# Keys and values stored to DRAM as whole fp32, split in two on GpSimd after they are read back

## The reference

```python
for n in (1, 2):
    h = layer_norm(x)
    q = h @ wq + bq;  k = ctx @ wk + bk;  v = ctx @ wv + bv        # 16 heads x 128
    k, v = concat(k, bias_k), concat(v, bias_v)                    # one more key and value
    x = x + concat_heads(softmax(q @ k.T / sqrt(128)) @ v) @ wo + bo
x = x + gelu(layer_norm(x) @ w_fc1 + b_fc1) @ w_fc2 + b_fc2
```

## Time and profile before

| | us |
|---|---|
| median of 3 runs | 2357.29 (2355.6 to 2358.11) |
| the profiled execution | 2355.32 |
| its span | 2353.5 |
| mean granted TensorE clock | 0.997 of full speed |
| PE busy | 2308.7 (98%) |
| DVE, ACT, POOL busy | 1488.8, 1177.4, 892.9 |

### The profile page before, as it was taken

How to read it: one execution, slowest core, us unless ns; L and a number is a source line. 1 busy time by engine, 2 the same in 40 slices (tenths; PEclk the granted TensorE clock), 3 DMA queues, 4 the chain that set the end, 5 groups by cost and what they waited for, 6 DMA issues and landing times.

```text
span 2353.5 us, 33519 instructions
## 1 busy us (share of the span) xinstructions
PE 2308.7 (98%) x12144; PEld 1961.7 (83%) x12144; DVE 1488.8 (63%) x2444; ACT 1177.4 (50%) x2897; POOL 892.9 (38%) x876
## 2 busy tenths in 40 slices
PE   7999999999999999999999999999999998999999
PEld 4888888788887788888888878888888887788887
DVE  4777767777777666666666776666666666534433
ACT  3322224322323866666666677666666667322222
POOL 5787876688786430011100253211101114611110
PEclk9999999999999999999999999999999999999999
DMA  4677775577777433333334323343334330100001
GB/s 169 233 269 271 266 278 198 197 251 280 268 267 252 159 121 134 131 126 123 138 121 141 126 85 124 133 141 125 117 126 143 128 134 29 34 30 27 28 1 72
DMA packets 147937, 352.88 MB, mean 150 GB/s; under 512 B 9536, under 2 KB 75584, under 8 KB 131392
## 3 DMA queue, kind: packets, MB, share of 16 engines
q1 hardware_dynamic: 147056, 350.65, 42.9%
q10 hardware_dynamic: 720, 0.10, 0.0%
HBM read 211.78 MB, written 138.94 MB: 149 GB/s over the span
## 4 chain that ended last, share of the span: by engine, by line
PE 87%; ACT 5%; DVE 3%; issue 2%; POOL 2%; DMA 0%; SPq 0%; DVEq 0%; ACTq 0%; POOLq 0%
PE U L781 22%; PE U L783 22%; PE U L782 22%; PE T L909 4%; PE O L781 2%; PE O L783 2%; PE S L783 2%; PE O L782 2%; PE S L781 2%; PE S L782 2%; ACT probs L1125 1%; ACT aff L1084 1%; POOL z L705 1%; ACT probs L1117 1%; DVE hT L1358 1%
## 5 line engine op out<-in xcount | busy, mean ns | idle before, releaser
L580 POOL CAST wos<-raw 128x1024 fp32r<-128x1024 f32 x20 | 20.9, 1047 | 852.9 <-PE U L783 852.9
L1377 DVE TENSOR_TENSOR x<-x,U 128x512 f32<-128x512 f32 x384 | 261.2, 683 | 80.8 <-PE U L783 78.6
L1385 DVE TENSOR_REDUCE nm<-S 128x2 f32<-128x514 f32 x256 | 177.3, 693 | 123.4 <-PE S L783 119.6
L1117 ACT ACTIVATE probs<-S,nm 128x257 f32<-128x257 f32 x512 | 237.7, 476 | 27.2 <-DVE nm L1385 27.2
L1135 ACT ACTIVATE PT<-T 128x512 fp32r<-128x512 f32 x256 | 152.5, 596 | 173.3 <-PE T L909 172.8
L1125 ACT ACTIVATE probs<-probs,rs 128x256 f32<-128x256 f32 x512 | 230.1, 500 | 0.5 <-DVE rs L1389 0.5
L1400 DVE SCALAR_TENSOR_TENSOR oT<-O,hc,oT 128x256 fp32r<-128x256 f32 x256 | 123.8, 484 | 143.1 <-ACT oT L1144 143.1
L781 PE MATMUL U<-wos,oT 128*128 128x512 f32 x512 | 213.4, 417 | 0.3 <-DVE gT L1368 0.2
L1072 ACT ACTIVATE stage<-tmp 128x512 fp32r<-128x512 f32 x128 | 81.1, 633 | 243.9 <-DVE tmp L1350 235.5
L783 PE MATMUL U<-wos,oT 128*128 128x512 f32 x512 | 202.0, 395 | 0.0
L1393 DVE TENSOR_TENSOR PT<-T,PT 128x512 fp32r<-128x512 f32 x256 | 175.5, 686 | 41.8 <-ACT PT L1135 41.8
(11 more groups left out here) (196 smaller groups left out, 6717.2 us busy)
## 6 DMA issues: line engine op xcount, KB each, us to landing
kd<-stage SPq DMA_DIRECT2D x128, 516.0 KB, 3.7
kb<-kd SPq DMA_DIRECT2D x64, 1032.0 KB, 4.8
vd<-stage SPq DMA_DIRECT2D x128, 512.0 KB, 5.2
vb<-vd SPq DMA_DIRECT2D x64, 1024.0 KB, 5.0
raw<-wk SPq DMA_DIRECT2D x32, 512.0 KB, 4.9
rawv<-wv SPq DMA_DIRECT2D x28, 512.0 KB, 6.2
raw<-wa SPq DMA_DIRECT2D x24, 512.0 KB, 5.9
raw<-wb SPq DMA_DIRECT2D x24, 512.0 KB, 5.9
```

Source lines behind the costliest of these rows:

```text
L1117: ins = act.activation(probs[:, r, qt, 0:257], S[:, qt, 0:257], ACT.Exp, bias=nm[:, r, qt:qt + 1], scale=-1.0, accum_out=sums[:, r, qt:qt ...
L1377: dve.tensor_tensor(x[:, tile, :], x[:, tile, :], bank(what, s, t), ALU.add).then_inc(free, 1)
L1385: dve.tensor_reduce(nm[:, J % 2, :], S[:, :, 0:257], AX.X, ALU.min).then_inc(least, 1)
```

## The change

Key blocks and value tiles are written to their slot by the DVE instruction that sums them (L1311, L1350 before), in fp32, and nothing is rounded or subtracted in the rounds. A slot and both DRAM tensors are half as large. When a step's keys have come back, into the lo half of `kb`, POOL rounds them into the hi half and subtracts in place (`split_keys`); the same for values (`split_values`). PE waits for POOL's subtraction instead of the DMA. POOL's list in the attention is written anew. `bkx` and its two instructions are gone. `z` holds key weights' sums in the rounds, and the temporaries of the openings lie where `wvs` lies, so some waits are other ones.

```diff
-        (stage,) = at(r, 16512, ("stage", [4, 2, 516], F32R))
+        (stage,) = at(r, 8256, ("stage", [4, 516], F32))
+        early_v = at(r + 8256, 8256, ("early_v0", [CH, 256], F32), ("early_v1", [CH, 256], F32))
...
+        (z,) = at(r, 8192, ("z", [4, D], F32))
+        ks = at(r, 8192, ("ks0", [4, 2, P], F32), ("ks1", [4, 2, P], F32))
...
             def load_k(s):
                 if s > 1:
                     sp.wait_ge(logit, 4 * (s - 2) + 4)
-                sp.dma_start(f(kbuf[s % 2][:]), kd[s // CHUNKS, s % CHUNKS]).then_inc(k_in[s % 2], 16)
+                sp.dma_start(f(kbuf[s % 2][:, 1]), kd[s // CHUNKS, s % CHUNKS]).then_inc(k_in[s % 2], 16)
...
-                    sp.wait_ge(staged, n + 1)
+                    sp.wait_ge(free, FREE["V", r, t] + 1)
+                    sp.dma_start(vd[r % GROUPS, tile // 4, :, :, tile % 4, :], by_body(value_slot(n))).then_inc(sent[n % 4], 16)
...
+            def split_keys(s):
+
+                hi_part_of, lo_part_of = kbuf[s % 2][:, 0], kbuf[s % 2][:, 1]
+                pool.wait_ge(k_in[s % 2], 16 * (s // 2 + 1))
+                pool.tensor_copy(hi_part_of, f(lo_part_of)).then_inc(k_hi, 1)
+                pool.wait_ge(k_hi, s + 1)
+                pool.tensor_tensor(lo_part_of, f(lo_part_of), f(hi_part_of), ALU.subtract).then_inc(k_lo, 1)
+
+            def split_values(s):
+
+                hi_part_of, lo_part_of = vbuf[s % 2][:, 0], vbuf[s % 2][:, 1]
+                pool.wait_ge(v_in[s % 2], 16 * (s // 2 + 1))
+                pool.tensor_copy(hi_part_of, f(lo_part_of)).then_inc(v_hi, 1)
+                pool.wait_ge(v_hi, s + 1)
+                pool.tensor_tensor(lo_part_of, f(lo_part_of), f(hi_part_of), ALU.subtract).then_inc(v_lo, 1)
...
             normalise(0, 0, (0, 1))
             queries(0)
+            split_keys(0)
             normalise(0, 1, (0, 1))
+            split_values(0)
             outputs(0)
             normalise(0, 2)
...
+            for s in range(STEPS):
+                E, c, n = s // CHUNKS, s % CHUNKS, s // CHUNKS // BODIES
+                first = s - n * BODIES * CHUNKS
+                if s + 1 < STEPS:
+                    split_keys(s + 1)
+                if E and c == 0:
+                    outputs(E)
+                if s + 1 < STEPS:
+                    split_values(s + 1)
+                if first == 0:
+                    normalise(n, 3)
+                if first > BODIES * CHUNKS - CHUNKS:
+                    normalise(n + 1, first - (BODIES * CHUNKS - CHUNKS) - 1)
+                if c == 0:
                     queries(E + 1)
+                if 2 <= first < 2 + CHUNKS:
+                    add_bias(n, first - 2)
...
                 if J % 4 == 0:
-                    pe.wait_ge(k_in[s % 2], 16 * (s // 2 + 1))
+                    pe.wait_ge(k_lo, s + 1)
...
                 if J % 4 == 0:
-                    pe.wait_ge(v_in[s % 2], 16 * (s // 2 + 1))
+                    pe.wait_ge(v_lo, s + 1)
...
-            act.activation(bkx[:, 0, :], hc[:, 2, :], ACT.Copy).then_inc(bk_hi, 1)
...
-                act.wait_ge(summed, 7 * quad(r, i) + MADE_BY[o])
-                act.activation(key_slot(0, n), by_batch(z[:, o, :]), ACT.Copy).then_inc(hi, 1)
-
-            def values(r, t):
-                n = KV["V", r, t]
-                act.wait_ge(free, FREE["V", r, t] + 1)
-                slot_free(n)
-                act.activation(value_slot(0, n), by_body(tmp[:, t % 2, :]), ACT.Copy).then_inc(hi, 1)
+                act.activation(bias_columns(n), hc[:, 2, at_:at_ + 1].unsqueeze(2).to_broadcast([P, 2, 2]), ACT.Copy).then_inc(edged, 1)
...
-                    for i in range(2):
+                    for i in range(4):
                         act.wait_ge(sent[i], 16 * len(KV) // 4)
                 act.activation(PT[:, J % 2, 0, :], T[:], ACT.Copy).then_inc(pt_hi, 1)
...
-                    dve.wait_ge(staged, KV["C", ROUNDS - 1, 1, C21] + 1)
+                    dve.wait_ge(k_form, 7 * 2 * ROUNDS)
...
+                    slot = KV["C", r, i, to]
+                    if slot >= 4:
+                        dve.wait_ge(sent[slot % 4], 16 * (slot // 4))
+                    dve.scalar_tensor_tensor(out=key_slot(slot), in0=by_batch(left), scalar=hc[:, 1, at_:at_ + 1],
+                                             in1=by_batch(right), op0=ALU.add, op1=op).then_inc(summed, 1)
...
-            def keys(r, i, o):
-                n = KV["C", r, i, o]
-                dve.wait_ge(hi, HI["C", r, i, o] + 1)
-                dve.tensor_tensor(key_slot(1, n), by_batch(z[:, o, :]), f(key_slot(0, n)), ALU.subtract).then_inc(staged, 1)
...
-                dve.tensor_tensor(tmp[:, t % 2, :], bank("V", r, t), vb[:].rearrange("p a n -> p (a n)"), ALU.add).then_inc(free, 1)
-                dve.wait_ge(free, FREE["V", r, t] + 1)
-                dve.wait_ge(hi, HI["V", r, t] + 1)
-                dve.tensor_tensor(value_slot(1, n), by_body(tmp[:, t % 2, :]), f(value_slot(0, n)), ALU.subtract).then_inc(staged, 1)
+                dve.tensor_tensor(value_slot(n), bank("V", r, t), vb[:].rearrange("p a n -> p (a n)"), ALU.add).then_inc(free, 1)
```

More of the change, by code:

```diff
@@ L438, in load_value_weights @@
                         sp.wait_ge(split_v[i], r)
[L439 to L442 removed]
+                    if e == 1:
                         sp.wait_ge(z_x, TILES // 2 * (r // GROUPS + 1))
@@ L594, in key_blocks @@
                         (2, 1): raw[i][:, 0:2, P:2 * P], (2, 2): raw[i][:, 2:4, P:2 * P]}
-            def key_sums(r, i):
-                early = r == 0 or (r, i) == (GROUPS, 1)
-                return [(early_s[i] if early else ks)[:, k] for k in range(4)]
             def sums(r, i):
@@ L604, in sums @@
                 a = key_blocks(i)
-                s1, s2, s3, s4 = key_sums(r, i)
+                s1, s2, s3, s4 = (ks[i][:, k] for k in range(4))
                 pool.wait_ge(raw_in[i], 16 * (r + 1))
@@ L1151, in _ @@
                 elif what == "C":
-                    keys(*a)
+                    bias_of_keys(*a)
                 elif what == "B":
@@ L1156, in _ @@
                     turned_context(*a)
-                elif what == "V":
-                    values(*a)
                 elif what == "Z":
@@ L1407, in _ @@
                     products(*a)
-                elif what == "C":
-                    keys(*a)
                 elif what == "B":
```

116 lines of the change are left out of this document (32 added, 84 removed).

## The result

| | before | changed |
|---|---|---|
| median of 20 runs, us | 2357.11 (2355.60 to 2360.44) | 2362.39 (2358.27 to 2368.88) |
| ratio to before | | 1.0021 (95% interval 1.0015 to 1.0028) |
| profiled execution, us | 2355.32 | 2363.07 |
| span of it | 2353.5 | 2361.2 |
| mean granted clock | 0.997 | 0.995 |

A forecast was written before the change was run, and what follows sets the result against it. PE was taken as the bound, busy 98% of the span, so only its waits could change. Terms -4.4 + 1.3 + 6.8 + 1.7 = +5.4 on 2355.3 gave 2360.7, plus 2.0 for the median: 2362.7, range 2353 to 2371.

The forecast's parts named there:

- Rounds, 0: Rounds: less ACT and DVE work and halved transfers gain nothing, as PE waits for none; 0, bounds 0 to +3.
- Round 15 into step 0, -4.4: Junction: `z` comes earlier without L1343, -2.7 of PE's wait and -1.7 of low clock; bounds 0 to -4.7.
- The start, +1.3: Kernel start: ACT's function table load moves from idle time behind the wait for PE's first block; bounds 0 and +1.3.
- Holds, +6.8: Layer starts: POOL's split subtractions hold DVE's row L1358 in steps 1, 30, 31, 33, 62; bounds 0 and +12.
- one tenth decides: Step 33: key subtraction at 1416.6 against L1358 at 1416.65, either 0 or +2.1; taken as +1.0.
- The clock, one drop more net, +1.7: Layer starts: longer PE waits bring one more drop to lower clock, net; bounds -1.7 and +5.
- The middle, 0: Middle of each layer: splits cost PE nothing, since DVE instructions there have a PSUM operand or are reductions.
- no hold: Rival, chance 0.12: splits miss DVE's rows at the layer starts and the junction is won, 2354.2.
- a gain in the rounds: Rival, chance 0.08: in the rounds a hidden pace of PE falls, some -9 us, 2348.
- a late POOL: Rival, chance 0.08: POOL's list runs late at two layer starts, with clock drops, 11 us, 2374.
- a price in all steps: Rival, chance 0.04: every POOL subtraction costs PE something in all 64 steps, 0.5 us a hold, 2420.
- Casts hold too: Rival, chance 0.04: POOL's casts also hold DVE, longer holds and two new meetings, +9.5 in all, 2372.

The follow-up runs named there:

- experiment 2: Changed kernel, with POOL's first normalising also waiting for DVE's last sum of key products: 2363.22 us, ratio to before 1.0025.
- experiment 1: Changed kernel plus one small ACT instruction at the start, so the function table loads in idle time: 2361.73 us.
- experiment 6: Kernel before the change, with POOL's output-weight subtraction in step 32 waiting for DVE's row subtraction: 2353.13 us, ratio 0.9981.
- Experiment 3: Changed kernel, with POOL's subtractions at the layer starts waiting until DVE's row subtraction has run: 2351.76 us, ratio to before 0.9981.
- experiment 8: Changed kernel, with POOL making each split's subtraction twice in steps 6 to 27 of each layer: 2360.03 us, ratio to before 1.0013.
- experiment 5: Separate measuring kernel, 80 trials of POOL and DVE instructions released together; DVE's two-SBUF-input form ended 0.54 us behind POOL's subtraction or cast.
- experiments 9 to 11: Changed kernel with layer-start waits and early function table, repeated: 2348.76 us; then with POOL's step 32 value subtraction waiting for `vpe`: 2348.88, without: 2349.32.

## Why the prediction was right, step by step

The median was forecast at 2362.7 and came at 2362.39. Median against median the forecast was +5.4 and the change +5.28 us. Between the two profiled executions, from which the terms below are read, it was +7.75: the one of before lies 1.8 us under its median, the changed one 0.7 over. That the medians agree to some tenths is luck, since terms here were off by 1 us and more, and a single stretch at half clock comes or doesn't.

- **Rounds, 0:** +0.03. Right.
- **Round 15 into step 0, -4.4:** -4.36 up to 748, the clock's part included. Right in place and size. Of its two reasons the removed L1343 alone gives all but 0.4 (experiment 2). "The earlier rows of ACT and DVE there gain nothing more" failed: PE gained another 1.78, mainly as its wait for `hT` at the end of the junction fell from 2.4 to 1.0. That the row at 745 took 0.69 instead of 2.08 is not the reason: in experiment 2 it took 1.79, and PE gained the same. Of this, 0.89 was given back where PE came earlier to the `z` of chunk 2 (that wait went from 0.5 to 1.4), and 0.2 more in step 0. Together -5.0.
- **The start, +1.3:** +2.36 in this profile, mis-sized by a term that the prediction left out. The load itself is right, +1.35 at 25 us. The other 1.1 came by 30 us in the longer stretch at half clock behind PE's wait (experiment 1). By the means of eleven profiles both together cost 1.6. Beside them the start scatters, also in a kernel that starts like before (-1.13 at 60 us, experiment 6). One place of it can be named: PE's wait ahead of L955 at 44 to 55 us, which the profile puts down to no engine, took 1.5 us before and in the changed kernel, and 2.6 in experiments 3 and 6. What sets that wait stays open.
- **Holds, +6.8:** the five meetings came where they were placed. The rows of steps 1, 30, 31 and 62, costed at 1.4 to 1.5, were 1.61, 1.48, 1.81 and 1.49 longer. PE lost 1.50 in step 1 and 1.49 in step 62. In step 30 it lost the hold and 1.3 of the lower clock; in step 31 the 1.81 less 0.64 that came back of it (in experiment 2 the row of step 31 met nothing, and PE gained 0.64 there behind the same stretch). The one where "one tenth decides" fell to the long side, 2.82 us at 1419.33, 2.13 for the 1.0 that I took. Together 8.4. Experiment 3 shows the cause. (My upper bound of +12 was added wrongly: seven holds of 2.2 less the 2.16 that is there are 13.2.)
- **The clock, one drop more net, +1.7:** two errors that nearly cancel. Behind the junction this profile has four stretches (1351, 1402, 1426, 1996), before had one, so three more instead of one. But each cost less than the 1.7 that I took, because PE makes up part of it at its next waits: 0.7 net at step 30, 1.0 at step 33, 0.3 behind step 62, together 2.0. Experiment 6 has the same for the old stretch in step 32: 1.6 saved, 0.65 lost again.
- **The middle, 0:** 0.00 in both layers, and with POOL's subtractions doubled (experiment 8). Its list of DVE's forms there left out the reciprocals, which read SBUF alone; they weren't held either.
- **"By the rows only the subtraction holds":** wrong. A cast holds as well, to 0.54 us behind its end (experiment 5; the row of 1.25 us at 1425.77). I had gone by rows beside the scaling, and of the three POOL instructions tried that is the one which lets DVE in early. For the cast the rule of the Trainium skill (SBUF — State Buffer, Who interferes with whom) was the better guide. It changed little here: casts met the second row of steps 1 and 33 (1.26 and 1.25 us), which before the change had met `add_bias` and taken 1.44 and 1.45.

The rivals: no hold, a gain in the rounds, a late POOL and a price in all steps are excluded by the rows and by experiments 3 and 8. "Casts hold too" was right in the mechanism and wrong in its price of +9.5, since the casts ahead of the subtractions were over when the rows began, and those behind them waited for DVE themselves (1.50 us for 1.04).

## What to carry to other kernels

Moving work to an engine that is half idle costs nothing by its busy time, but by what it locks: before giving GpSimd elementwise work, list VectorE's instructions with two SBUF inputs, and its fp32 scalings from SBUF, on the critical chain, and order the two engines there by a wait. Waits in place of a chance meeting also made the time steadier, 2347.9 to 2350.8 us in 15 executions against 2358 to 2369 in 20. After a gain, look where it is given back: of 6.1 us won at the junction, step 0 took 1.1.

## What the runs showed of the hardware

- A held VectorE instruction ends at a fixed distance behind GpSimd's end, whenever it started: 0.54 us for two SBUF inputs of 512, 0.28 for the fp32 scaling, beside a subtraction and beside a cast; forms with a PSUM operand never differ from their time alone, nor do reciprocals of two numbers (0.17 us at most, experiment 8).
- Length is no protection: an fp32 scaling of four numbers took 1.19 us beside GpSimd's subtraction, 0.17 alone (experiments 9 to 11).
- GpSimd's scaling with two columns (2.07 us for 128x512) holds only for its first part: VectorE is through 1.31 us behind its start (two SBUF inputs) or 1.04 (fp32 scaling).
- The lock is mutual: GpSimd's subtraction took 2.85 us for 2.34 when VectorE's two-input form was first. VectorE's fp32 scaling, though 0.04 us ahead, was itself the one that was held.
- A difference of about 1 us in the position of two engines turns a meeting of 0.9 us into one of 2.4, and PE's loss there from 0.9 to 3.0 us with the half-clock stretch ahead of it that made the difference (experiment 2).
- The same hold is followed by a stretch at half clock (3.4 or 6.8 us) in some profiles and not in others (experiment 8), and a stretch of 3.4 us costs PE 0.3 to 1.0 us net at the layer starts, where waits follow it, and 1.6 in round 15. So a single trace says little about the mean over executions.
